# A two-expert feed-forward pass: gathered 128-token tiles replaced by a dense pass over transposed activations

## What is computed

```python
x = x + tanh(g_xattn) * (fake_quant(layernorm(x)) @ fake_quant(ctx))       # per batch, 512x1024 @ 1024x1024
t = layernorm(x)                                                           # 1024 tokens
scores = softmax(t @ router_w + router_b) + router_bias                    # 16 experts in 4 groups
# the two best groups are kept, of them the two best experts; gate holds their scores, zero elsewhere
for e in 16 experts:                                                       # ew1, ew2: 1024x256, ew3: 256x1024
    h = silu(t @ ew1[e] + eb1[e]) * (t @ ew2[e] + eb2[e])
    y += gate[:, e] * (h @ ew3[e] + eb3[e])
z = (silu(t @ sw1 + sb1) * (t @ sw2 + sb2)) @ sw3 + sb3                    # shared expert, 512 inner columns
x = x + tanh(g_ffn) * (y + z)
```

## Time and profile before

| | us |
|---|---|
| median of 3 runs | 409.54 |
| lowest and highest run | 407.63, 411.38 |
| span of the profiled execution, first to last instruction | 405.0 |
| median less that span | 4.54 |
| PE busy in the span | 346.4 |

### The profile page before, as it was taken

How to read it: one execution, slowest core, us unless ns; L and a number is a source line. 1 busy time by engine, 2 the same in 40 slices (tenths; PEclk the granted TensorE clock), 3 DMA queues, 4 the chain that set the end, 5 groups by cost and what they waited for, 6 DMA issues and landing times.

```text
span 405.0 us, 6929 instructions
## 1 busy us (share of the span) xinstructions
PE 346.4 (86%) x2070; PEld 161.6 (40%) x2071; DVE 193.3 (48%) x402; ACT 155.8 (38%) x220; POOL 62.1 (15%) x66
## 2 busy tenths in 40 slices
PE   0588798999999999979996899997786959999750
PEld 0243798445433644433332334443232414444210
DVE  3887958679884487654477411110146231111100
ACT  2793578775259201110443321222436242222220
POOL 4101201000220000002011022222211221322211
PEclk9999899999999999999999689999898989999965
DMA  7993564694099300009984778699977759778953
GB/s 299 390 349 30 178 189 159 160 322 142 0 209 284 132 2 1 0 10 372 313 292 104 210 131 171 129 273 267 303 177 155 211 98 154 160 150 170 175 128 52
DMA packets 80664, 71.38 MB, mean 176 GB/s; under 512 B 53014, under 2 KB 69470, under 8 KB 80640
## 3 DMA queue, kind: packets, MB, share of 16 engines
q1 hardware_dynamic: 38148, 43.29, 34.1%
q0 software_dynamic: 5040, 18.35, 20.1%
q10 hardware_dynamic: 37452, 9.44, 12.6%
HBM read 41.71 MB, written 16.78 MB: 144 GB/s over the span
## 4 chain that ended last, share of the span: by engine, by line
PE 54%; DMA 12%; DVE 11%; ACTq 8%; ACT 7%; issue 5%; POOL 1%; DVEq 1%; POOLq 0%
PE PS L1384 15%; PE PS L1419 11%; PE PS L1586 9%; DMA out_dram<-rows,row 6%; ACTq L703 6%; PE PS L1331 5%; PE PS L1563 4%; DMA area<-split_dram,tok 3%; DVE stats L806 2%; DMA area<-area 2%; PE PS L1400 2%; ACT areaW L689 2%; PE PS L1421 1%; ACTq L268 1%; DMA sc<-in_g_ffn_dram 1%
## 5 line engine op out<-in xcount | busy, mean ns | idle before, releaser
L1586 PE MATMUL PS<-areaW,area 128*128 128x512 f16 x384 | 88.9, 390 | 0.3 <-DVE areaW L1212 0.3
L1384 PE MATMUL PS<-areaT,areaW 128*128 128x512 f16 x288 | 62.6, 379 | 1.4 <-DVE SA L891 1.4
L1563 PE MATMUL PS<-areaT,areaH 128*128 128x512 f16 x192 | 54.3, 426 | 7.6 <-ACT rows L735 4.6
L1586 PEld LDWEIGHTS PS<-areaW,area 128*128 128x128 f16 x384 | 37.5, 100 | 45.1 <-issue 4.5
L1419 PE MATMUL PS<-SW,areaH 128*128 128x512 f16 x192 | 44.2, 380 | 2.3 <-DVE areaH L896 2.3
L493 POOL DMA_INDIRECT out_dram<-rows,row x16 | 25.4, 1589 | 121.9 <-issue 72.2
L1384 PEld LDWEIGHTS PS<-areaT,areaW 128*128 128x128 f16 x288 | 28.0, 98 | 34.8 <-DVE SA L891 1.6
L474 POOL DMA_INDIRECT area<-split_dram,tok x19 | 19.6, 1031 | 110.2 <-ACT tok L708 63.1
L1232 DVE COPY areaH<-PS 128x512 f16<-128x512 f16 x16 | 6.8, 424 | 54.5 <-issue 52.8
L1331 PE MATMUL PS<-area,areaQ 128*128 128x512 f16 x128 | 31.2, 395 | 0.6 <-DVE area L843 0.5
L1563 PEld LDWEIGHTS PS<-areaT,areaH 128*128 128x128 f16 x192 | 17.6, 105 | 34.5 <-issue 21.2
(11 more groups left out here) (222 smaller groups left out, 412.0 us busy)
## 6 DMA issues: line engine op xcount, KB each, us to landing
ring<-in_L_ffn_sw_dram SPq DMA_DIRECT2D x12, 512.0 KB, 5.8
X<-in_x_dram SPq DMA_DIRECT2D x8, 512.0 KB, 5.8
areaT<-in_ctx_dram SPq DMA_DIRECT2D x8, 512.0 KB, 10.1
ring<-in_ctx_dram SPq DMA_DIRECT2D x8, 512.0 KB, 4.3
out_dram<-X SPq DMA_DIRECT2D x8, 512.0 KB, 4.4
areaT<-in_L_ffn_ew_dram SPq DMA_DIRECT2D x4, 1024.0 KB
wrow<-in_L_ffn_ew_dram SPq DMA_DIRECT2D x4, 1024.0 KB, 6.0
ring<-in_L_ffn_ew_dram SPq DMA_DIRECT2D x4, 1024.0 KB, 7.7
```

The lines of the kernel that those rows point to most:

```text
L1384: last = mm(PS[:, 4 + 2 * (c % 2) + w, lo:hi], SW[:, wp, 2 * c + w, k, :], XT[:, xp, k, tk], start=(k == 0 and n == 0), stop=(k == KC - 1 ...
L1563: mm(PS[:, h, :], HTS[1 - j][:, hp, c, :], W3S[1 - j][:, wp, c, hs], start=(c == 0 and n == 0), stop=False)
L1586: mm(PS[:, 4 + j, :], XGT[j][:, xp, k, :], W12S[j][:, wp, k, :], start=(k == 0 and n == 0), stop=False)
```

## The change

The token lists, the gather, the transposes of gathered tokens, the scatter and the store of the parts go. The two experts of lowest number that any token chose are run over all tokens, from XT, which holds all tokens transposed. Experts beyond two run in a loop, `Fori(SLOTS, n)`, where `n` is the number of chosen experts.

- `list_experts` replaces the `place_` functions: from the 16 counts it makes `EL` and `n`. `gate_column` and `split_gates` make the gate of each token for the two experts and its two f16 parts.
- POOL makes eight diagonal blocks of 128x512 from the gates, and PE multiplies them with ones (8 matmuls), so that a PSUM bank holds the gates of 512 tokens in every partition. ACT copies these to GR.
- `expert_up(u)`, u from 0 to 7 (expert, batch, half of the inner columns): 48 matmuls with weights stationary and 512 tokens moving. h comes out transposed. ACT makes silu with the bias, POOL multiplies by GR, DVE adds the other bias and multiplies, ACT and DVE make the two parts.
- `tile_down(i)` makes all down products of a tile in one PSUM group per half: four blocks of experts, and for tiles 4 to 7 the four of the shared expert, too. So `shared_down(4..7)` goes, but its matmuls don't.
- The bias matmuls go: the inner biases are per partition now, and the outer ones, with `r1`, are added to X by DVE in `finish_rows` (3 instructions of 128x1024 per tile), which takes the place of ACT's `add_r1` (L598).
- The result is added to X by DVE and stored from there.
- Weights: four quarters of two DMAs of 256 KB, one f32 buffer (the ring); the second expert's quarters are loaded as the first's are split.

```diff
 # PE, in the second batch's shared_up
+                if c == 2:
+                    pe.wait_ge(dg_rdy, 4 * SLOTS)
+                    pe.wait_ge(el_rdy, 1)
+                    pe.wait_ge(su_hf, SC + 2)
+                    for idx in range(2 * SLOTS):
+                        for h in range(2):
+                            last = mm(PS[:, idx, :], onesh[:, :],
+                                      DG[:, idx // B, h, idx % B, :, :].rearrange("p t n -> p (t n)"), start=(h == 0),
+                                      stop=(h == 1))
+                        last.then_inc(g_done, 1)
...
+            def expert_up(u):
+                j, b, c = u // 4, u // 2 % 2, u % 2
...
+                for w in range(2):
+                    cs = slice(w * INTER + c * P, w * INTER + (c + 1) * P)
+                    for k in range(KC):
...
+                        for n, (wp, xp) in enumerate(((0, 0), (0, 1), (1, 0))):
+                            last = mm(PS[:, EU_BANK[u] + w, :], W12S[j][:, wp, k, cs], XT[:, xp, k, b * S:(b + 1) * S],
+                                      start=(k == 0 and n == 0), stop=(k == KC - 1 and n == 2))
+                last.then_inc(eu_done, 1)
+            for u in range(8):
+                expert_up(u)
+            n = chosen(pe)
+            pe.wait_ge(eu_hf, 8)
+            with pe.Fori(SLOTS, n) as a:
...
+            def tile_down(i):
...
+                    parts = [(HE[b], q, W3S[q // HC], q % HC) for q in range(SLOTS * HC)]
+                    if b == 1:
+                        parts = [(HT, c, SW3, c) for c in range(SC)] + parts
+                    for s, (ht, q, w3, c) in enumerate(parts):
+                        for m, (hp, wp) in enumerate(((0, 0), (1, 0), (0, 1))):
+                            last = mm(PS[:, DN_BANK[i] + h, :], ht[:, hp, q, ts], w3[:, wp, c, hs],
+                                      start=(s == 0 and m == 0), stop=(s == len(parts) - 1 and m == 2))
+                    last.then_inc(dn_done, 1)
 # GpSimd
+            pool.wait_ge(gate_rdy, 1)
+            pool.wait_ge(at_done, NT)
+            for j in range(SLOTS):
+                for h in range(2):
+                    for b in range(B):
+                        nc.gpsimd.tensor_tensor(DG[:, j, h, b, :, :], idh[:, :].unsqueeze(1).to_broadcast([P, TB, P]),
+                                                gsp[:, h, j, b * TB:(b + 1) * TB].unsqueeze(2).to_broadcast([P, TB, P]),
+                                                ALU.mult).then_inc(dg_rdy, 1)
+            def gate_unit(u):
+                j, b = u // 4, u // 2 % 2
+                pool.wait_ge(g_rdy, 2 * j + b + 1)
+                pool.wait_ge(eu_silu, u + 1)
+                nc.gpsimd.tensor_tensor(SA[:, u % 2, :], SA[:, u % 2, :], GR[:, j, b, :], ALU.mult).then_inc(eu_gated, 1)
 # SP
+            n = chosen(sp)
+            for j in range(2, TB):
+                sp.wait_ge(xt_in[j], 16)
+            e0, e1 = expert_of(0), expert_of(1)
+            load_bias_columns(e0, 0, eb_in[0])
+            for q in range(4):
+                load_up_quarter(e0, q, w12_in[q])
+            load_bias_columns(e1, 1, eb_in[1])
+            for j, e in enumerate((e0, e1)):
+                load_row(e, j, b3_in)
+            for q in range(4):
+                sp.wait_ge(w12_lo, q + 1)
+                load_up_quarter(e1, q, w12_in[q])
+            for j, e in enumerate((e0, e1)):
+                sp.wait_ge(w12_lo, 4 + 2 * j + 2)
+                load_down(e, j, w3_in[j])
 # DVE, from the end of the router on
             route()
             su_dve(SC)
-            place_experts()
+            list_experts()
+            for j in range(SLOTS):
+                gate_column(j, sel[:, j:j + 1, :])
+            split_gates(slice(0, SLOTS)).then_inc(gate_rdy, 1)
             su_dve(SC + 1)
-            place_positions()
+            shared_row()
+            for q in range(4):
+                low_quarter(w12_hi, q + 1, 0, q, w12_lo)
             su_dve(SC + 2)
-            place_slots()
             su_dve(SC + 3)
...
+            for q in range(4):
+                low_quarter(w12_hi, 4 + q + 1, 1, q, w12_lo)
+            for u in range(8):
+                eu_gate(u)
+                eu_low(u)
+                if u in (2, 3):
+                    low_down(u - 2)
+                for i in {0: (0,), 1: (1,), 4: (2, 3), 5: (4, 5), 6: (6, 7)}.get(u, ()):
+                    finish_rows(i)
...
+            for i in range(NT):
+                tile_out(i)
```

More of the change, by code:

```diff
@@ L325, in turn_tokens @@
                     .then_inc(xt_in[i - TB], 16)
[L327 to L336, removed]
+            for r in range(4, 12):
                 load_chunk(r)
@@ new lines, in gate_unit @@
+            def gate_unit(u):
[4 more added lines that the diff above has]
+            for u in range(8):
+                gate_unit(u)
+            n = chosen(pool)
+            with pool.Fori(SLOTS, n) as a:
+                pool.wait_ge(xg_rdy, 2 * a - 2)
+                pool.sem_inc(further, 1)
+                for u in range(4):
+                    pool.wait_ge(xu_silu, 4 * a - 8 + u + 1)
+                    nc.gpsimd.tensor_tensor(SA[:, u % 2, :], SA[:, u % 2, :], GR[:, 0, u // 2, :], ALU.mult)\
+                        .then_inc(xu_gated, 1)
@@ L592, in evac_q1 @@
                 nc.scalar.activation(Q1T[:, i, :, :], bank16(2 + i % 2), ACT.Copy).then_inc(q1_rdy, 1)
-            def add_r1(b):
-                act.wait_ge(r1_rdy, b + 1)
-                for i in range(b * TB, b * TB + TB):
-                    nc.scalar.activation(X[:, i, :], X[:, i, :], ACT.Identity, bias=r1[:, i:i + 1]).then_inc(x_r1, 1)
             def tk_hi_evac(i):
@@ L665, in _ @@
             quant_ctx(1, 7)
-            for j in range(2):
-                act.wait_ge(split_out[j], 16 * TB // 2)
+            act.wait_ge(tk_T, 2 * TB)
             su_silu_of(3)
@@ L675, in _, with split_up_quarter @@
                 ln_rows(i)
-            add_r1(0)
-            add_r1(1)
             act.wait_ge(lg_sub, 1)
-            nc.scalar.activation(t1[:, :, :], lg[:, :, :], ACT.Exp).then_inc(lg_exp, 1)
-            for c in range(SC):
+            nc.scalar.activation(spread[:, :, :], lg[:, :, :], ACT.Exp).then_inc(lg_exp, 1)
+            def split_up_quarter(signal, count, got, j, q):
+                act.wait_ge(signal, count)
+                ks = slice(2 * q, 2 * q + 2)
+                nc.scalar.activation(W12S[j][:, 0, ks, :], W12F[:, ks, :], ACT.Copy, scale=WS).then_inc(got, 1)
@@ new lines, in gate_rows, with eu_silu_of @@
+            def gate_rows(idx, done, count, dst, got):
+                act.wait_ge(done, count)
+                nc.scalar.activation(dst, PS[:, idx, :], ACT.Copy, scale=1.0 / GS).then_inc(got, 1)
+            def eu_silu_of(u):
+                j, q = u // 4, u // 4 * HC + u % 2
+                act.wait_ge(eu_done, u + 1)
+                if u == 0:
+                    act.wait_ge(su_lo, 2 * SC)
+                if u % 4 == 0:
+                    act.wait_ge(eb_in[j], 32)
+                if u >= 2:
+                    act.wait_ge(eu_lo, u - 1)
+                nc.scalar.activation(SA[:, u % 2, :], PS[:, EU_BANK[u], :], ACT.Silu, bias=ebc[:, j, 0, u % 2:u % 2 + 1],
+                                     scale=1.0 / UPS).then_inc(eu_silu, 1)
@@ L681, in _, with eu_hi_of @@
+            def eu_hi_of(u):
+                j, b, c = u // 4, u // 2 % 2, u % 2
+                act.wait_ge(eu_hf, u + 1)
+                nc.scalar.activation(HE[b][:, 0, j * HC + c, :], SA[:, u % 2, :], ACT.Copy, scale=HS / UPS)\
+                    .then_inc(eu_hi, 1)
+            for c in range(2):
                 su_silu_of(SC + c)
                 su_hi_of(SC + c)
-            def split_up(loads, j):
-                act.wait_ge(w12_in[j], 32 * loads)
-                for q in range(4):
-                    nc.scalar.activation(W12S[j][:, 0, 2 * q:2 * q + 2, :], W12F[j][:, 2 * q:2 * q + 2, :], ACT.Copy,
-                                         scale=WS).then_inc(w12_hi[j], 1)
@@ new lines, in _ @@
+            su_silu_of(SC + 2)
+            su_hi_of(SC + 2)
+            for idx in range(2 * SLOTS):
+                gate_rows(idx, g_done, idx + 1, GR[:, idx // B, idx % B, :], g_rdy)
+            su_silu_of(SC + 3)
+            su_hi_of(SC + 3)
+            act.wait_ge(su_done, 2 * SC)
+            for q in range(4):
+                split_up_quarter(w12_in[q], 64, w12_hi, 1, q)
+            for u in range(8):
+                eu_silu_of(u)
+                eu_hi_of(u)
+                if u in (2, 3):
+                    j = u - 2
+                    act.wait_ge(w3_in[j], 16)
+                    for q in range(HC):
+                        nc.scalar.activation(W3S[j][:, 0, q, :], W3F[j][:, q, :], ACT.Copy, scale=WS).then_inc(w3_hi, 1)
@@ L1534, in _ @@
-            pe.wait_ge(empty_rdy, 1)
-            shared_down(NT - 1)
-            pe.wait_ge(sd_read, NT - 1)
```

(15 more changed lines are left out.)

871 lines of the change are left out of this document (292 added, 579 removed).

## The result

The changed kernel takes 428.04 us (median of 4 runs), the one before 409.41 in the same comparison. The ratio on record is 1.043, with a 95% interval of 1.038 to 1.049 (the two medians alone give 1.046). Forecast were 349 us, with a range of 336 to 362. The change is slower, and the forecast was wrong in sign.

What follows compares the result with a forecast made beforehand. PE's work bounds the kernel up to 206 us, then a mix of it and token traffic. PE's work 326.1, gates 4 + 2, loop 5.5 + 2.5, tail 4.3 gave span 344.4; plus 4.5, 349 us (336 to 362).

Steps and rivals of the forecast that it cites:

- Second wait added: the loop: Between up and down products PE waits for the last gated unit: 5.5 us (3.1 to 11.6), plus 2.5 of clock.
- Rival C: The loop runs because some token chose a third expert: a pass costs 83 us, time 432, slower; chance 0.02.
- the sum: PE's work to 326.1 us, plus waits, lower clock and ending: span 344.4, with 4.5 around it 349.
- Rival A: POOL is quick: no PE wait for gates, 3.1 us before down products, clock stays: 337.5 us; chance 0.24.
- The first wait: Before the gate matmuls PE waits for POOL's eight diagonals: 4 us (0 to 13.6), plus 2 for a lower clock.
- The tail: After PE's last product DVE adds the last half tile, SP issues, 256 KB land: 4.3 us with hops.

## Why the prediction was wrong, point by point

**The step that failed** is a half sentence in "Second wait added: the loop": that PE waits for `eu_hf` 8 "also when the loop runs no time", and with it the whole sum, which gives the loop no pass. With two experts the loop runs once. Rival C had nearly the right price under a wrong condition. It put a pass at 83 us and the time at 432, and measured were 428.04; but C's chance of 0.02 was argued from whether a third expert exists. There are two experts, as the rows of the weight loads said, and the number 2 costs a pass all the same. That 432 lies so near is luck in part: the time without a pass was put 11.6 us too high (349 against 337.39), and the pass 7.7 too low (83 against 90.7). The question to ask was not how many experts there are but what the loop does when there is nothing to do. Nothing in the kernel of before could answer it: its loops have constant ends that are above their starts.

**The price of a pass** is 93.95 us from two passes (93.6 in the trace, from the gate products of the first at 270.24 to those of the second at 363.87), and 424.5 - 335.4 = 89.1 of span against the tested loop, where the wait stays. The 83 lacked three things: the wait for DVE's diagonals (6.85 us), the gate products (1.89), and the lower clock behind each pause (44.5 us for the up products counted at 41.5, 24.0 for the down products counted at 21.6). Its 12 us for weights were more than the 8.5 seen, and its 8 for the tail of the units and of ew3 was right (7.93).

**The rest of the sum** can be held against the run with the loop behind a test, which is the kernel that the forecast described. It takes 337.39 us, near the lower end of the range. Rival A had 337.5 for it, and this is luck, too: A was right that PE doesn't wait for the gates, but it had 3.1 us and no clock for the second wait, where 8.1 and 2.7 were measured, and 326.1 us of PE's work, where 335.4 - 8.1 - 2.7 - 3.2 = 321.4 is left; its tail is 3.8 us, where the sum has 4.3, without a reason. The span was to be 344.4 and is 335.4. Of the 9 us:

- PE reaches the up products at 176.0, not 178.5. Removing eight bias matmuls gave more than their 0.32 us each: PE's 96 products of the first `shared_down` took 20.72 us, where they and the bias matmuls had taken 24.0 (110.57 to 134.58), 3.3 instead of 2.6. A further 1.7 us was there at the start of these products (108.91 against 110.57 us). It fits the 64 matmuls of 128 columns shown above: they took 5.36 us at a granted clock of 0.68 in the kernel before and 3.73 at 1.00 in the changed one. Such a drop shows up at this place in other runs too, among them runs without the loop, so I don't count it to the change: 1.7 of the 2.5 us say nothing about the sum.
- The first wait was 0, not 4 with 2 of clock. The eight POOL products took 9.90 us, where I took 11.2 and some 3 more for being held. Both parts of that were too large: a product by itself took 1.04 us, not 1.4, and meeting DVE added 1.9 us to the eight, not up to 5.3. The rows that made me fear a hold were right that the two meet and that POOL pays; they don't show that DVE pays as well, 2.06 us for a quarter instead of 1.22. The estimate from the figure in the Trainium skill's "GPSIMD Engine Reference", § 3.1, was 1.1 us for one product; 1.04 us were measured. Its § 8 names contention with VectorE instructions that have two SBUF inputs; the trace agrees, with 2.02 us for a POOL product beside such a one.
- The second wait was 8.1 us and 2.7 of clock (23.56 against 20.88 us for 96 products), where I took 5.5 and 2.5. Half of the gap comes with test and jump, for which I had 1.2 and let some of it pass under the wait.
- The down products take 62.3 us without a drop of the clock (260.60 to 322.92 in the run without the loop), 0.216 us each. I counted 0.225, the pace of 12 products that alternate with a bias matmul. That pace belonged to the pair, not to the down form: 2.4 us.
- The tail behind the last product is 3.2 us, not 4.3.

In sum -2.5 - 6 + 2.8 - 2.4 - 1.1 = -9.2 us, against 335.4 - 344.4 = -9.0.

**What held:** the weights of both experts are in place without a pause of PE, the up stage of 384 products has none and takes 82.9 us, and `finish_rows` delays the last unit's chain by a microsecond: in the run with the test the last gated unit comes 4.1 us behind the last up product, where the chain alone was put at 3.1.

## What to carry to other kernels

A loop with an end known only at run time needs one question before any other: what does it do at zero passes? Here it runs once, silently, since its pass adds zero; put it behind a test, and force the number by hand to see each case. A wait placed ahead of such a loop, for the loop's sake, belongs behind the test as well: it cost 7.7 us of time, and 10.3 by the traces, with the jump that it laid open. And an estimate for a rival must be joined to the right trigger: a price of 83 us deserves the code to be read for every way of reaching it, not only for the one that the data speak against.

## What the runs showed of the hardware

A test with a jump over a long loop cost 0.48 us of PE's time right behind queued products, and about 4 us right behind a wait, 8.12 against 4.17. Behind PE's pauses of 3 us and more the granted clock was lower for some microseconds, as in before: 0.69 in the stretch behind the 8.12 us in this window of the run with the test,

```profile
267.20:276.00 8.80, 8.80 (x29) 3.42 (x30) 1.50 (x2) 0.00 (x0) 0.00 (x0) 0.69 0.01 2
```

and 0.50 while PE made the gate products behind the 10.75 us. Outside the loop such a pause cost 1.7 to 2.7 us more than its length: 22.6, 22.58 and 23.56 us for 96 products behind pauses of 3.0, 4.17 and 8.12 us, instead of 20.88, and 2.6 us behind the 10.75. Behind the 0.48 us nothing was lost (20.88). A DVE instruction with two inputs in SBUF and a POOL product, side by side, lengthened each other: 1.22 to 2.06 us for the one, 1.04 to 2.02 for the other.
